# Projecting queries and own keys in 7 tiles of 128 tokens a group in place of 8 batches of 112

## The reference, cut to what matters

```
ln  = layernorm(layernorm(x)) * ln_w + ln_b
q   = LN(fp8_linear(ln, wq));  qx = LN(fp8_linear(ln, wqx))     # 16 heads of 128
k   = LN(fp8_linear(ln, wk));  v  = fp8_linear(ln, wv)           # 8 key heads of 128
core = softmax(q k' / sqrt(128)) v                               # within the batch, 112 tokens
kx, vx = split(ctx @ w_kv_x);  kx = LN(kx)                       # 375 context tokens a batch
xout = softmax(qx kx' / sqrt(128)) vx
x  = x + tanh(g) * (fp8(concat(core, xout)) @ wproj) * scales
```

## Time and profile before

| | |
|---|---|
| median of three runs | 1267.72 us |
| the profiled execution | 1270.7 us, of which the span is 1268.9 us |
| PE busy | 1125.3 us, 89% of the span |
| DVE busy | 862.6 us, 68% |
| ACT busy | 698.3 us, 55% |
| POOL busy | 481.8 us, 38% |
| mean granted clock of PE | 0.955 of full speed |

### The profile page before, as it was taken

How to read it: one execution, slowest core, us unless ns; L and a number is a source line. 1 busy time by engine, 2 the same in 40 slices (tenths; PEclk the granted TensorE clock), 3 DMA queues, 4 the chain that set the end, 5 groups by cost and what they waited for, 6 DMA issues and landing times. The chain is left out here.

```text
span 1268.9 us, 22397 instructions
## 1 busy us (share of the span) xinstructions
PE 1125.3 (89%) x5792; PEld 909.2 (72%) x5792; DVE 862.6 (68%) x1740; ACT 698.3 (55%) x1746; POOL 481.8 (38%) x608
## 2 busy tenths in 40 slices
PE   1089999979999998999998999998799939999996
PEld 1068777767787776778776888886688727777775
DVE  7978778886778787887888778777444765655100
ACT  7965677854666784566776556555112413334442
POOL 3074344343344434443444444442000222655432
PEclk9599999999999999999999999999899859999998
DMA  5041111114111112411111311110546066766220
GB/s 192 20 173 46 32 39 49 41 33 167 32 55 40 33 32 61 162 41 31 48 43 30 132 37 51 40 36 11 182 142 240 22 227 191 217 183 188 46 42 1
DMA packets 51715, 107.36 MB, mean 85 GB/s; under 512 B 5984, under 2 KB 26464, under 8 KB 49568
## 3 DMA queue, kind: packets, MB, share of 16 engines
q1 hardware_dynamic: 46912, 97.00, 23.5%
q0 software_dynamic: 4704, 9.18, 3.3%
HBM read 91.48 MB, written 16.52 MB: 85 GB/s over the span
## 5 line engine op out<-in xcount | busy, mean ns | idle before, releaser
L721 PE MATMUL p_proj<-w_hi,xqs 128*112 128x256 f32 (+1 forms) x512 | 173.4, 358 | 57.0 <-DVE w_lo L495 47.7
L569 POOL TENSOR_TENSOR c_lo<-c_raw,c_hi 128x500 fp32r<-128x500 f32 x96 | 122.4, 1275 | 175.4 <-ACT c_hi L609 175.4
L730 PE MATMUL p_proj<-w_hi,c_hi 128*125 128x512 f32 x384 | 166.2, 433 | 9.3 <-DVE w_lo L495 8.2
L559 POOL TENSOR_TENSOR va<-ss,epst 112x4 f32<-112x4 f32 (+2 forms) x192 | 74.1, 386 | 261.7 <-DVE ss L862 261.7
L721 PE MATMUL p_proj<-w_lo,xqs 128*112 128x256 f32 (+1 forms) x512 | 163.7, 339 | 0.0
L563 POOL TENSOR_TENSOR rs<-va,mhalf 112x4 f32<-112x4 f32 (+2 forms) x192 | 155.5, 810 | 18.0 <-POOL va L559 5.8
L730 PE MATMUL p_proj<-w_hi,c_lo 128*125 128x512 f32 x384 | 152.6, 397 | 0.0
L730 PE MATMUL p_proj<-w_lo,c_hi 128*125 128x512 f32 x384 | 152.4, 397 | 0.0
L721 PEld LDWEIGHTS p_proj<-w_hi,xqs 128*112 128x112 f32 x512 | 90.1, 176 | 73.7 <-issue 55.6
L862 DVE TENSOR_REDUCE ss<-sq 112x4 f32<-112x512 f32 (+2 forms) x192 | 96.2, 504 | 52.6 <-ACT sq L630 51.7
L658 ACT ACTIVATE pcross<-p_cross,nmax 112x375 f32<-112x375 f32 x128 | 73.2, 574 | 82.7 <-DVE nmax L891 82.0
(11 more groups left out here) (230 smaller groups left out, 2720.6 us busy)
## 6 DMA issues: line engine op xcount, KB each, us to landing
c_raw<-in_ctxT SPq DMA_DIRECT2D x96, 250.0 KB, 2.6
shared<-in_w_in SPq DMA_DIRECT2D x16, 1024.0 KB, 9.1
shared<-in_wproj SPq DMA_DIRECT2D x32, 256.0 KB, 2.9
raw_g<-in_Wg SPq DMA_DIRECT2D x8, 1024.0 KB, 6.6
raw_u<-in_Wu SPq DMA_DIRECT2D x8, 1024.0 KB, 7.6
raw_d<-in_Wd SPq DMA_DIRECT2D x8, 1024.0 KB, 5.6
cat_scratch<-cat SPq DMA_DIRECT2D x32, 224.0 KB, 2.0
shared<-cat_scratch SPq DMA_DIRECT2D x2, 1792.0 KB, 8.0
```

The lines of the kernel that those rows point to most:

```text
L559: pool.tensor_tensor(va[0:rows, lo:hi], ss[0:rows, lo:hi], epst[0:rows, lo:hi], ALU.add).then_inc(va_done, 1)
L569: pool.tensor_tensor(flat(c_lo[:, k, :, :]), flat(c_raw[:, k, :, :]), flat(c_hi[:, k, :, :]).bitcast(F32), ALU.subtract).then_inc(cl_done, 1)
L721: m = pe.matmul(bank[0:T, o:o + w], xqs[:, n, k, :], (w_hi, w_lo)[i % 2][:, k, lo:lo + w], start=(i == 0), stop=(i == 2 * KB - 1))
L730: m = pe.matmul(bank[0:CT, :], a[:, ch, k, :], w[:, k, CKX:CV], start=(i == 0), stop=(i == 3 * KB - 1))
```

## The change

Queries, own keys and the queries of the context are now projected for tiles of 128 tokens, cut from the 896 tokens without regard to batches: a group has 7 tiles (`TJ`), taken in steps u=0 to 6. Values and context stay by batch, 8 a group. The step u=7 has no tile: PE projects only the 8 matmuls of v and the three context chunks there, and ACT, DVE and POOL have no nq, nqx and nk to take. The step that attends batch 7 has no transposes of them.

- `qT`, `qxT` and `kT` have two slots, by the parity of the batch. Tile u holds the last tokens of batch u and the first 16(u+1) of batch u+1, so `turned` 0, 1 and 2 are two activations each: one for batch u, one for batch u+1.
- `inputs` writes three casts of 128 tokens and one of 112; for u=7 only the last.
- `USED` has five parts, k and v apart. `w_high` 0, 1 and 2 (q, qx, k) are issued in step u=6 ("queries") behind takes 3, 4 and 5, `w_high` 3 (v) in u=7 ("keys"), `w_high` 4 (context) at the start of the next group ("new").
- `w_low` on DVE: 0 in u=6, 1 and 2 in u=7, 3 and 4 in "new". In the very first step POOL does 2 and 3, DVE 0, 1 and 4.
- Centring is in steps u=2, 3, 4 and 5.
- Step u=7 has an order of its own on PE, ACT and DVE (`last_step`).
- The inner loops are gone: the loop over the groups has 8 steps written out, the last group follows in line. The semaphore counts go by the functions `pj_no`, `st_no`, `tr_no` and `td_no`, which count what steps with and without a tile contribute.
- c_high and c_low of u=7's first chunk are issued at the end of u=6.

The diff, cut:

```
-USED = (((CQ, CQX),), ((CQX, CK),), ((CK, CKX), (CV, 2048)), ((CKX, CV),))
+USED = ((CQ, CQX), (CQX, CK), (CK, CKX), (CV, WC), (CKX, CV))
...
+def has_tile(pos):
+    return pos[1] < TJ
...
+        step(FIRST, None, 0, "first", None)
         with eng.Fori(0, GP - 1) as gp:
-            batches(gp)
-            step(gp * B + B, 0, gp * B + 7, gp + 1, "new", None)
...
+            for u in range(1, B):
+                k = u - 2 if 2 <= u < 2 + KB else None
+                step((gp, u), (gp, u - 1), gp + 1, {TJ - 1: "queries", B - 1: "keys"}.get(u), k)
+            step((gp + 1, 0), (gp, B - 1), gp + 1, "new", None)
+        for u in range(1, B):
+            step((GP - 1, u), (GP - 1, u - 1), None, None, None)
+        step(None, (GP - 1, B - 1), None, None, None)
...
 POOL, step
+            if has_tile(s):
+                for j in range(3):
+                    c_low(s, j)
+                    rstd(s, j)
+                for j in range(3, 6):
+                    rstd(s, j)
+                if s[1] == TJ - 1:
+                    c_low((s[0], B - 1), 0)
+            else:
+                c_low(s, 1)
+                rstd(s, 3)
+                c_low(s, 2)
+                rstd(s, 4)
+                rstd(s, 5)
...
 ACT, turned (n < 3)
+            own = T - (P - T) * u
+            act.activation(dst[:, u % 2, :, T - own:T], src[:, :, 0:own], ACT.Identity, bias=b, scale=w)
+            act.activation(dst[:, 1 - u % 2, :, 0:P - own], src[:, :, own:P], ACT.Identity, bias=b,
+                           scale=w).then_inc(t_done, 1)
...
 ACT, the step u=7
+            turned(t, 0)
+            turned(t, 1)
+            take(s, 2)
+            turned(t, 2)
+            turned(t, 3)
+            c_high(s, 1)
+            take(s, 3)
+            exp_self(t)
+            exp_cross(t, 0)
+            exp_cross(t, 1)
+            turned(t, 4)
+            c_high(s, 2)
+            if change == "keys": w_high(g, 3, change)
+            take(s, 4)
+            exp_cross(t, 2)
+            exp_cross(t, 3)
+            take(s, 5)
...
 ACT, step
-            if change == "old": w_high(g, 0)
...
+            if change == "queries": w_high(g, 0, change)
+            if A: take(s, 4)
             if k is not None: weights.centre(act, g, k, 1)
+            if change == "queries": w_high(g, 1, change)
+            if A: take(s, 5)
             if k is not None: weights.centre(act, g, k, 2)
+            if change == "queries": w_high(g, 2, change)
+            if A and s[1] == TJ - 1: c_high((s[0], B - 1), 0)
...
 PE, the step u=7
+            turn(t, 0)
+            turn(t, 1)
+            project(s, 2)
+            turn(t, 2)
+            turn(t, 3)
+            project(s, 3)
+            score_self(t)
+            score_cross(t, 0)
+            score_cross(t, 1)
+            turn(t, 4)
+            project(s, 4)
+            turn_self(t)
+            turn_cross(t, 0)
+            score_cross(t, 2)
+            turn_cross(t, 1)
+            score_cross(t, 3)
+            project(s, 5)
+            outputs(t, 0)
+            turn_cross(t, 2)
+            turn_cross(t, 3)
+            outputs(t, 1)
...
 DVE, the step u=7
+            if change == "keys": w_low(g, 1)
+            sums(s, 3)
+            max_self(t)
+            scale(s, 3)
+            max_cross(t, 0)
+            max_cross(t, 1)
+            norm_self(t)
+            norm_cross(t, 0)
+            norm_cross(t, 1)
+            take_self(t)
+            sums(s, 4)
+            take_cross(t, 0)
+            max_cross(t, 2)
+            scale(s, 4)
+            take_cross(t, 1)
+            max_cross(t, 3)
+            if change == "keys": inputs((s[0] + 1, 0))
+            norm_cross(t, 2)
+            norm_cross(t, 3)
+            if change == "keys": w_low(g, 2)
+            smoothed(t, 0)
+            take_cross(t, 2)
+            take_cross(t, 3)
+            sums(s, 5)
+            smoothed(t, 1)
+            scale(s, 5)
+            rounded(t)
...
 DVE, step
+            if change == "new": w_low(g, 3)
             if A: sums(s, 0)
+            if change == "new": w_low(g, 4)
             if A: sums(s, 1)
...
-            if change == "old": w_low(g, 0)
...
-            if change == "old": w_low(g, 1)
+            if change == "queries": w_low(g, 0)
             if A: sums(s, 5)
             if A: scale(s, 5)
-            if change == "old": w_low(g, 2)
```

More of the change, by code:

```diff
@@ L466, in passes @@
     def passes(eng, step):
[L470 to L480, removed]
-        with eng.Fori(0, GP - 1) as gp:
-            batches(gp)
-            step(gp * B + B, 0, gp * B + 7, gp + 1, "new", None)
[L485 to L491, removed]
+        step(FIRST, None, 0, "first", None)
+        with eng.Fori(0, GP - 1) as gp:
+            for u in range(1, B):
[5 more added lines that the diff above has]
+        step(None, (GP - 1, B - 1), None, None, None)
     def split_low(eng, n):
[L494 to L497, removed]
+        lo, hi = USED[n]
+        return eng.tensor_tensor(w_lo[:, :, lo:hi], w_raw[:, :, lo:hi], w_hi[:, :, lo:hi].bitcast(F32), ALU.subtract)
     @block.sync
@@ L609, in c_high, with squares @@
+            act.wait_ge(pj_rdy, pj_no(before(s), 3 + k))
             act.activation(flat(c_hi[:, k, :, :]), flat(c_raw[:, k, :, :]), ACT.Copy).then_inc(ch_done, 1)
-        def take(s, j, par):
-            bank = p_proj[:, j % 2, :]
-            act.wait_ge(pj_rdy, 6 * (s + 1) + j + 1)
-            act.wait_ge(tr_rdy, 10 * s + (j + 1 if j < 3 else 5))
+        def squares(s, j, rows, n):
+            if j >= 2 and (has_tile(s) or j == 5):
+                act.wait_ge(rd_done, st_no(s, j - 2))
+            elif not has_tile(s):
+                act.wait_ge(rd_done, st_no(before(s), {3: 5, 4: 4}[j]))
+            else:
+                act.wait_ge(rd_done, st_no(before(s), 4 + j))
+            act.activation(sq[0:rows, j % 2, 0:n], p_proj[0:rows, j % 2, 0:n], ACT.Square,
+                           scale=float(HD) ** -0.5).then_inc(pj_done, 1)
@@ L617, in take @@
+        def take(s, j):
+            bank, par = p_proj[:, j % 2, :], s[1] % 2
+            act.wait_ge(pj_rdy, pj_no(s, j))
+            if j >= 3:
+                act.wait_ge(tr_rdy, tr_no(before(s), 4))
+            elif has_tile(s) and s is not FIRST:
+                act.wait_ge(tr_rdy, tr_no(tile_before(s), j))
             if j < 2:
-                act.activation((nq, nqx)[j][0:T, :], bank[0:T, :], ACT.Copy)
-                n, rows = 512, T
+                act.activation((nq, nqx)[j][:, :], bank, ACT.Copy)
+                squares(s, j, P, 512)
@@ L620, in take @@
             elif j == 2:
-                act.wait_ge(ou_rdy, 2 * s)
-                act.activation(nk[0:T, :], bank[0:T, 0:256], ACT.Copy)
-                act.activation(val[0:T, par, :], bank[0:T, 256:512], ACT.Copy)
-                n, rows = 256, T
+                act.wait_ge(ou_rdy, 2 * lin(s))
+                own = act.activation(val[0:T, par, :], bank[0:T, 256:512], ACT.Copy)
+                if has_tile(s):
+                    act.activation(nk[:, :], bank[:, 0:256], ACT.Copy)
+                    squares(s, j, P, 256)
+                else:
+                    own.then_inc(pj_done, 1)
@@ L694, in step @@
                 for j in range(6):
-                    take(s, j, par)
+                    take(s, j)
         passes(act, step)
@@ L798, in outputs, with last_step, step @@
             m.then_inc(ou_rdy, 1)
-        def step(s, par, t, g, change, k):
+        def last_step(s, t):
+            turn(t, 0)
[19 more added lines that the diff above has]
+            outputs(t, 1)
+        def step(s, t, g, change, k):
             A, Q = s is not None, t is not None
+            Qt = Q and has_tile(t)
+            if A and not has_tile(s):
+                return last_step(s, t)
             if change not in ("first", "new"):
@@ L953, in step @@
             if A: scale(s, 2)
-            if A and b_next is not None: inputs(s + 1, b_next)
+            if A: inputs((s[0], s[1] + 1))
             if Q: norm_cross(t, 2)
```

315 lines of the change are left out of this document (168 added, 147 removed).

## The result

The changed kernel takes 1280.00 us (median of 6 runs, 1274.14 to 1282.46), the kernel before 1267.81 beside it (6 runs): ratio 1.0083, interval 1.0055 to 1.0111. It is slower, and the forecast of 1260 had the wrong sign; 1280 lies outside the range.

A forecast was written before the change was run, and what follows sets the result against it. PE was taken to bound plain steps, with w_lo pauses at weight changes. Pairs -24.9, u=7 +7.5, u=2 to 6 +10.4 and smaller terms gave -7.7: 1270.7 to 1263.0 profiled, 1260.0 against the median; range 1249 to 1275.

The forecast's parts named there:

- the slower one: Rival: DVE's chain in u=7 and the group start outlasts the old pause; u=7 at 31, total 1277.5 us, chance 0.20.
- a dearer second activation: Part of the slower rival: 0.44 us for each second activation on ACT, +0.3 in each of 24 steps, 7 us.
- three pairs u=0, u=1: Group starts without the old weight-change pause: pairs of 60.4, 58.9, 56.4 become 50.4, 50.4, 49.9 us, -24.9.
- u=2 to 6, three groups: Steps with second activations and moved centring: 127.4 us against 123.9 a group, +10.4 over three groups.
- last u=7: Last group's step u=7 without new weights: 21.4 us for 23.9, -2.5.
- drain: Work behind the last u=7, ruled by a chain that only starts earlier: -1.5 us.
- Step u=7, 'keys': Step without a tile, with new weights: 27.5 us for 25.0, bounds 21 and 31, +7.5 over three groups.
- The pause of 3.5: In u=7 PE waits 3.5 us before turn(t, 3) for DVE's scale, late behind w_lo of the queries.
- the 3.2 behind the max: In u=7, the time from DVE's max of the self scores to PE's self transposes: 3.2 us.
- the clock at +1.0: Whole kernel: 1.0 us added back, because u=7 has a PE pause as long as the old ones.
- the tax: Second activations on ACT make PE wait, 0.29 us taken for each; plain steps +0.58.
- the listed waits of 0.4 to 0.6: Sign of being right: PE waits 0.4 to 0.6 us for ACT's squares before 256-wide matmuls in u=1 to 6.

The follow-up runs named there:

- e7: Changed kernel with 24 more 256-column matmuls, results overwritten, on PE in its pause before turn(t, 3) of each u=7; 1273.6 us.
- e1: Changed kernel with turn(t, 4) on PE moved right behind turn(t, 3), before project(s, 3), in u=7; 1275.2 us.
- e5: e3 with DVE's w_lo 1 moved behind take_self and ACT's w_high 3 behind take(5) in u=7; 1262.7 us.
- e3: Changed kernel with the moves of e1 and e2, and c_high and c_low of batch 7's chunk 0 issued earlier in u=6; 1264.0 us.
- e6: Changed kernel with w_lo 1 in u=7 computed for 16 columns only, the other 496 left out; 1279.2 us.
- e8: e5 with qT as a ring, so tile 0 takes two activations only in u=3 and u=6; 1255.9 us.
- e11: e5 with w_lo 1 behind max_cross(t, 3), w_lo 2 behind take_cross, qT and qxT as rings, and buffers reused or narrowed for room; 1249.05 us.
- e2: Changed kernel with DVE's w_lo 0 in u=6 moved behind sums(5) and scale(5); 1272.8 us.
- e12: Changed kernel with the two rings and room edits of e11 but none of its reordering; 1272.5 us.

## Why the prediction was wrong

It forecast a gain of 7.7 us and the kernel lost. Of its rivals the slower one (1277.5, chance 0.20) had the place right, u=7 at 31 us (31.6 on average), but 7 of its 17.5 us were a dearer second activation, which did not come; that its total is near 1280 is partly luck. Term by term, in the profiled executions' own time:

| term | predicted | measured |
|---|---|---|
| three pairs u=0, u=1 | 150.7 | 51.8 + 52.1 + 49.6 = 153.4 |
| u=2 to 6, three groups | 382.2 | 381.2 |
| plain step | 24.5 | 24.4 |
| **u=7 with new weights, three** | **82.5** | **94.7** |
| last u=7 | 21.4 | 26.0 |
| drain | 16.3 | 13.6 |
| whole attention stage | -7.7 | +8.4 |

The failed step is "Step u=7, 'keys'": 12.2 of the 16.1 us by which the stage is off, and its sibling at the end is 4.6 more; the pairs (+2.7) and the drain (-2.7) cancel. Inside it the count went wrong between the start of project(s, 3) and the max of the self scores, in three steps as follows:

| piece of u=7 | predicted | measured |
|---|---|---|
| start of the step to project(s, 3) | 6.5 | 6.90, 6.90, 6.89 |
| project(s, 3) | 2.9 | 4.14, 5.21, 5.03 |
| its end to the max of the self scores | 2.1 | 3.87, 3.88, 3.87 |
| max to the self transposes | 3.2 | 3.31, 3.30, 3.31 |
| the rest | 12.2 | 12.23, 13.62, 12.23 |

- The pause of 3.5 (measured 3.88), the 3.2 behind the max and the rest were right, but for 1.4 us in the second step, where the clock was low again in its last 2.4 us (0.50).
- project(s, 3) was to end at 9.4. In the last step it ended at 11.9, of which 2.2 is the half clock (e7). The prediction put the clock at +1.0 for the whole kernel, from the pauses of the kernel before; it missed that a pause right ahead of a long projection charges that projection too.
- The max was to come at 11.5 to 12. It came at 15.8, since take(s, 3) waited for turn(t, 4): with the wait gone the piece is 1.6 (e1). This wait could be read from the code; the sum took take(s, 3) as free, as it is in a plain step, where turn(t, 4) stands ahead of project(s, 3).
- DVE's scale was to take 0.4 and took 1.45 beside c_lo. The prediction had the collision for the rounding operations and for w_lo 1, and added 0 to 1.6 us; it hit the scale as well, on which PE was waiting. That cost is small, since project(s, 3) still starts within 0.4 us of the count. That a DVE and a POOL instruction of this kind shut each other out, the rule that it cited from the Trainium skill ("SBUF — State Buffer", "Who interferes with whom"), is borne out: in e5 c_lo takes 3.46 for 1.25. Which of the two waits, the second to issue by that rule, the starts do not bear out (see the last section).

The 27.5 that the forecast took for u=7 is what e3 measures in each of its three steps, with the max at 12.0 us, behind w_lo 1 as counted. So the count of DVE's order was sound, for a kernel in which the wait for turn(t, 4) and the low clock ahead of the max are gone; since e3 also has a shorter pause, 1.3 us, the agreement to 0.1 is in part chance.

The clock also varies between executions of the same code. The last u=7 has one code and one pause of 1.86 us ahead of turn(t, 3) in the changed kernel and in e6: it took 26.0 us at a clock of 1.00 there and 27.6 at 0.94 here, with project(s, 3) at 2.88 and 4.46. So the lengths of single steps carry 1 to 2 us of this, and no profiled execution accounts for the whole 12.2 us between the medians.

The range failed there too: its high end was u=7 at 30.5 with a tax of 0.85, where 31.6 came with 0.54.

Right were: the waits for w_lo go; the pairs become 7 to 9 us shorter (u=0 was 26.2, 27.1 and 25.2 where 24.6 was taken, 4.6 us in sum, and the step behind it 1.9 us shorter than taken); the tax, 0.54 for 0.58 in a plain step, and 127.0 for 127.4 in u=2 to 6, where e8 and e11 confirm its cause, 0.26 for each second activation where 0.29 was taken. The tax does not show as the listed waits of 0.4 to 0.6 that the prediction named as its sign: the row has 0.16 and the view at most 0.4, while the matmul starts 0.55 later. The drain got 4.2 us shorter, not 1.5.

That it costs the order and not the work is shown from both sides: e6 takes 2.1 us of DVE work out of each step and gains 0.8 in all, e3 takes no work out and gains 16. With both side effects mended the change is worth 21 us on the kernel before (e11), where PE work removed alone was counted at 23.2. No run gives the kernel before a better order of its own w_lo, so how much of the 21 that alone would bring is not shown.

Open is also how the gain of e3 divides between its edits. e1 gives 5.2 and e2 8.6 us in u=7, more together than the 12.2 of e3, and each of them also shifts what the clock does.

## What to carry to other kernels

When work is removed from the busiest engine in one step, write down for every other engine what each instruction there waits for in the new order, the buffers that it overwrites as well as its data: here the engine that lost work then stood waiting in the same step for nkx, pself, pcross and pcrossT. Look first at what stands right behind a new pause of PE: at half clock it pays once more. A buffer layout that makes one instruction into two is a price per step, and a ring that wraps seldom pays it seldom (e11: two steps in eight).

## What the runs showed of the hardware

- A c_lo that takes 1.25 us elsewhere, begun on POOL 0.08 us before a w_lo on DVE, took 3.46 us, while the w_lo kept its 2.28 (e5). In the changed kernel a c_lo begun 0.11 us before a w_lo kept its 1.31, and the w_lo took 3.34; in two steps of e12, begun 0.01 us before, the c_lo took 3.41 and the w_lo 2.28. Which of the two pays isn't told by the profile's start times. The Trainium skill ("SBUF — State Buffer", "Who interferes with whom") has it that the first to issue keeps the port; by the starts in e5 that would be c_lo, and c_lo it was that waited.
- In e6 a subtraction on 64 elements a lane took 1.28 us on DVE, with a c_lo on POOL beside it.
- In and behind a pause of 3.9 us on PE the granted clock was at 0.50 for 6.8 us (661.50 to 668.30), and 12 matmuls took 5.03 us for 2.85; with PE filled in the pause they ran at full clock in all three steps (e7). Adding matmuls made the kernel faster. Behind a pause of 1.86 us the same matmuls took 2.88 us in one execution and 4.46 in another (the last u=7 of the changed kernel and of e6).
- ACT pays by the instruction: 384 columns out of PSUM took 0.67 us, 128 took 0.45 and 64 took 0.42 to 0.43, and a second one behind the first costs 0.26 us of the step (e8). The Trainium skill ("ScalarE: Activation LUTs", "What ACT_TABLE_LOAD costs") gives a fixed part of 280 ns with one pointer operand, 93 ns for each further one, and an overlap of 93 ns back to back. By that a second activation on the same columns costs an estimated 0.28 us, and the trace agrees.
